# Two 64-wide self-attention blocks: transposed scores and column sums replaced by normalised weights that TensorE turns

## What is computed

```python
q = (xn @ q_w + q_b).reshape(b, s, H, HD).transpose(0, 2, 1, 3)     # H = 16, HD = 64, s = 512
k = (xn @ k_w + k_b).reshape(b, s, H, HD).transpose(0, 2, 1, 3)
v = (xn @ v_w + v_b).reshape(b, s, H, HD).transpose(0, 2, 1, 3)
q, k = _rope(q, theta), _rope(k, theta)                              # B1 only
scores = jnp.einsum('bhqd,bhkd->bhqk', q, k) * scale                 # scale = 1/8
scores = jnp.where(causal, scores, -jnp.inf)                         # B1 only
attn = jax.nn.softmax(scores, axis=-1)
ctx = jnp.einsum('bhqk,bhkd->bhqd', attn, v)
attn_out = ctx.transpose(0, 2, 1, 3).reshape(b, s, H * HD) @ o_w + o_b + xn
```

## Time and profile before

| what | us |
|---|---|
| median of three runs | 2612.14 |
| lowest and highest of them | 2607.64, 2616.47 |
| profiled execution, first to last instruction (its span) | 2602.9 |
| PE busy in it | 2223.6 (85%) |
| DVE busy | 1696.5 (65%) |
| ACT busy | 1135.9 (44%) |
| mean granted TensorE clock | 0.928 of full speed |

### The profile page before, as it was taken

The page is one execution under the profiler, slowest core; times in us unless marked ns, Lnnn a source line. Parts: engine busy times, 40 slices in busy tenths (PEclk is TensorE's granted clock), DMA queues, the critical chain, the costliest instruction groups (busy, mean ns, idle before and its releaser), DMA issues.

```text
span 2602.9 us, 32241 instructions
## 1 busy us (share of the span) xinstructions
PE 2223.6 (85%) x11288; PEld 882.6 (34%) x11288; DVE 1696.5 (65%) x3941; ACT 1135.9 (44%) x1859; POOL 143.0 (5%) x143
## 2 busy tenths in 40 slices
PE   7999979889999898887887888788788878867898
PEld 3333333533333564223323222332322233232433
DVE  5767758646566687765774676577567557754464
ACT  3333323112223333563665466365546636654411
POOL 0000000011110201000000000000000000010000
PEclk9999989789999898888999799799979979988999
DMA  4000000200000100000000010010001000030000
GB/s 145 1 1 1 1 1 1 96 19 1 1 1 1 52 21 25 25 1 25 24 20 1 25 43 1 25 37 7 3 23 43 1 25 26 2 102 1 1 1 8
DMA packets 38032, 54.33 MB, mean 21 GB/s; under 512 B 5073, under 2 KB 34546, under 8 KB 36338
## 3 DMA queue, kind: packets, MB, share of 16 engines
q1 hardware_dynamic: 37874, 52.28, 6.4%
HBM read 32.34 MB, written 0.52 MB: 13 GB/s over the span
## 4 chain that ended last, share of the span: by engine, by line
PE 38%; DVE 10%; ACT 8%; issue 4%; SPq 1%; DMA 0%; ACTq 0%; DVEq 0%
PE ps L2084 7%; PE ps L2064 5%; ACT big L2569 4%; PE ps L2045 4%; DVE C_nm L2746 3%; PE ps L2212 2%; PE ps L2129 2%; PE ps L2319 2%; PE ps L2224 2%; ACT big L2649 2%; PE ps L2315 2%; PE ps L2340 2%; PE ps L2231 2%; PE ps L2240 2%; PE ps L2189 1%
## 5 line engine op out<-in xcount | busy, mean ns | idle before, releaser
L2746 DVE TENSOR_REDUCE C_nm<-ps 128x1 f32<-128x512 f32 x768 | 501.9, 685 | 185.6 <-PE ps L2045 180.9
L2569 ACT ACTIVATE big<-ps 128x512 f32<-128x512 f32 x768 | 427.7, 595 | 234.3 <-PE ps L2064 225.0
L2045 PE MATMUL ps<-C_attn 62*128 62x512 bf16 x768 | 276.5, 417 | 62.6 <-DVE C_nm L2746 51.6
L2064 PE MATMUL ps<-C_attn 64*128 64x512 bf16 x768 | 253.7, 398 | 62.1 <-ACT big L2569 51.8
L2084 PE MATMUL ps<-big,C_attn 128*32 128x512 f32 x1536 | 212.8, 627 | 13.3 <-ACT big L2569 13.3
L2045 PEld LDWEIGHTS ps<-C_attn 62*128 62x128 bf16 x768 | 63.2, 94 | 304.1 <-DVE C_nm L2746 165.7
L2064 PEld LDWEIGHTS ps<-C_attn 64*128 64x128 bf16 x768 | 59.3, 93 | 274.9 <-ACT big L2569 204.1
L2649 ACT ACTIVATE big<-ps,C_biasx 77x512 f32<-77x512 f32 x192 | 115.6, 679 | 56.4 <-PE ps L2216 56.3
L861 DVE TENSOR_REDUCE A_nm<-ps 128x2 f32<-128x1024 f32 x64 | 77.8, 1215 | 85.8 <-PE ps L609 85.5
L787 ACT ACTIVATE A_p<-ps 128x1024 f32<-128x1024 f32 x64 | 65.6, 1025 | 110.2 <-PE ps L637 110.2
L787 ACT ACTIVATE B_p<-ps 128x1024 f32<-128x1024 f32 (+1 forms) x64 | 45.0, 703 | 149.7 <-PE ps L641 149.7
(11 more groups left out here) (414 smaller groups left out, 3787.5 us busy)
## 6 DMA issues: line engine op xcount, KB each, us to landing
C_attn<-C_first SPq DMA_DIRECT2D x144, 128.0 KB, 2.4
C_w<-in_C_w SPq DMA_DIRECT2D x6, 1090.0 KB, 5.0
C_attn<-in_D_ew SPq DMA_DIRECT2D x4, 1536.0 KB, 10.9
big<-in_B_ew SPq DMA_DIRECT2D x8, 514.0 KB
normw_later<-in_norm_w SPq DMA_DIRECT2D x1, 2304.0 KB, 16.3
A_w<-in_A_w SPq DMA_DIRECT2D x2, 1024.0 KB, 11.6
A_w<-in_A_w SPq DMA_DIRECT2D x2, 768.0 KB, 8.6
B_w<-in_B_w SPq DMA_DIRECT2D x1, 1536.0 KB, 11.2
```

Source lines behind the costliest of these rows:

```text
L2045: pe.matmul(ps[:, bank, :], lhsT=qs[side(hp, MAX_ROW), b, 2 * q + pq, t * P:(t + 1) * P], rhs=ks[side(hp, MAX_ROW), b, 2 * q + pq, :], sta ...
L2064: pe.matmul(ps[:, bank, :], lhsT=ks[side(1 - hp, HALF), b, 2 * q + pq, kt * P:(kt + 1) * P], rhs=qs[side(1 - hp, HALF), b, 2 * q + pq, :], ...
L2569: act.activation(prob[:, kt % 2, pq, 1 - hp, :], ps[:, bank, :], ACT.Exp, scale=SCALE)\
L2746: dve.tensor_reduce(nm[:, q % 2, t, pq, hp:hp + 1], ps[:, bank, :], AX.X, ALU.max, negate=True).then_inc(emptied[bank], 1)
```

## The change

`self_attention_block` is rewritten; A1 and B1 both use it. The unit of work is now a **step** i = (unit n, tile t of 128 queries), 64 in all. The scores are made once (`scores`), into one of two pairs of banks. DVE takes the row maxima. ACT takes the exponential of each head's rows by itself, with the negative maximum as its bias and with the row's sum as a second output. DVE inverts the two sums of each row and multiplies the rows by them in place (`weights`). PE turns the normalised rows in blocks of 128 x 128 (`turn`), ACT copies the turned blocks from PSUM (`copy_turned`), and PE makes the weighted sums of the 128 queries (`weigh`), one step behind the turning. ACT copies a unit's context (in B1 it adds the bias), `project_out` makes the output of each unit with tokens as rows, and DVE adds it to y unit by unit (`add_out`).

`split_max`, `turn_max`, `scores_T`, `add_up`, `denominators`, `invert`, `normalise`, `copy_out` and `turn_out` are gone. DVE, not ACT, copies queries and keys in A1 and multiplies the queries by 1/8 on the way; in B1 the tables of the queries carry the 1/8. Three banks (4, 5, 7) form a ring: projections, turned blocks and outputs take the next bank in turn, and PE waits until the bank's last content was taken.

```diff
+            def fill(key):
+                bank = RING[len(turns) % len(RING)]
+                turns.append(key)
+                uses[bank] += 1
+                place[key] = bank, uses[bank]
+                if uses[bank] > 1:
+                    pe.wait_ge(emptied[bank], uses[bank] - 1)
+                return bank
...
+            def turn(i):
+                n, t = divmod(i, TB)
+                pe.wait_ge(p_ready, 2 * (i + 1))
+                for key, heads in turned(i):
+                    bank = fill(key)
+                    for j, h in enumerate(heads):
+                        for kt in range(keys(t) // P):
+                            col = j * keys(t) + kt * P
+                            last = pe.transpose(ps[:, bank, col:col + P], prob[:, i % 2, h, kt * P:(kt + 1) * P],
+                                                m.ident[:])
+                    last.then_inc(filled[bank], 1)
+
+            def weigh(i):
...
+                for kt in range(keys(t) // P):
+                    for h in range(2):
+                        last = pe.matmul(ps[half(h), PV_BANK, t * P:(t + 1) * P], lhsT=v[:, n % 4, kt, half(h)],
+                                         rhs=probT[:, i % 2, kt, h, :], start=kt == 0, stop=kt == keys(t) // P - 1)
...
+            for i in range(STEPS):
+                n, t = divmod(i, TB)
+                if i + 2 < STEPS:
+                    scores(i + 2)
+                turn(i)
+                if i:
+                    weigh(i - 1)
+                if n + 2 < N:
+                    for what in at_step[t]:
+                        project(n + 2, what)
+                if t == TB - 1 and n:
+                    project_out(n - 1)
...
         @block.scalar
+            for i in range(STEPS):
+                n, t = divmod(i, TB)
+                copy_turned(i)
+                if t == 0 and n:
+                    copy_context(n - 1)
+                if t == 2 and n + 2 < N:
+                    copy_v(n + 2)
+                if i + 2 < STEPS:
+                    exps(i + 2)
...
         @block.vector
+            for i in range(STEPS):
+                n, t = divmod(i, TB)
+                if n + 2 < N and t in (1, 2):
+                    for what in at_step[t - 1]:
+                        take(n + 2, what)
+                if i + 2 < STEPS:
+                    row_max(i + 2)
+                if i + 1 < STEPS:
+                    weights(i + 1)
+                if t == 0 and n >= 2:
+                    add_out(n - 2)
```

More of the change, by code:

```diff
@@ new lines, in _, with project @@
+            ring.fill = fill
+            def project(n, what):
+                if n not in begun:
+                    begun.append(n)
+                    for (first, _), loaded in zip(W_PARTS, w_loaded):
+                        if first == n:
+                            pe.wait_ge(loaded, 16)
+                    if n == PAIRS and opening is not None:
+                        drained(pe, "turn_norm")
+                bank = fill((what, n))
+                if what == "v":
+                    for t in range(TB):
+                        last = pe.matmul(ps[:, bank, t * P:(t + 1) * P], lhsT=hT(n)[:, t * P:(t + 1) * P],
+                                         rhs=weight(n, WV), start=True, stop=True)
+                else:
+                    last = pe.matmul(ps[:, bank, :], lhsT=weight(n, column[what]), rhs=hT(n), start=True, stop=True)
+                last.then_inc(filled[bank], 1)
@@ L757, in _ @@
-            weigh(N - 1, TB - 1)
-            project_out(N - 2)
-            denominators(N - 1)
-            project_out(N - 1)
-            if tail is not None:
-                tail.tensor(pe, N, 0, S_BANK)
-            else:
-                for b in range(B):
-                    turn_out(b, S_BANK + b)
+            for what in pieces:
+                project(0, what)
+            for i in range(2):
+                scores(i)
+                project(i, "v")
+            for what in pieces:
+                project(1, what)
@@ new lines, in exps @@
+            def exps(i):
+                n, t = divmod(i, TB)
+                act.wait_ge(max_done, i + 1)
+                if i >= 2:
+                    for key, _ in turned(i - 2):
+                        arrived(act, key)
+                for h in range(2):
+                    act.activation(prob[:, i % 2, h, 0:keys(t)], ps[:, S_BANK + 2 * (i % 2) + h, 0:keys(t)], ACT.Exp,
+                                   bias=nm[:, i % 2, h:h + 1], accum_out=sums[:, i % 2, h:h + 1]).then_inc(exp_done, 1)
@@ new lines, in copy_turned @@
+            def copy_turned(i):
+                n, t = divmod(i, TB)
+                if i >= 2:
+                    act.wait_ge(pv_done, i - 1)
+                for key, heads in turned(i):
+                    bank = arrived(act, key)
+                    out = probT[:, i % 2, 0:keys(t) // P, heads[0]:heads[-1] + 1, :]
+                    act.activation(out.rearrange("p k h q -> p h k q"), ps[:, bank, 0:len(heads) * keys(t)]
+                                   .rearrange("p (h k q) -> p h k q", h=len(heads), q=P), ACT.Copy)\
+                        .then_inc(emptied[bank], 1)
@@ new lines, in weights, with add_out @@
+            def weights(i):
+                n, t = divmod(i, TB)
+                dve.wait_ge(exp_done, 2 * (i + 1))
+                c.after(dve.reciprocal(inv[:, i % 2, :], sums[:, i % 2, :]))
+                for h in range(2):
+                    row = prob[:, i % 2, h, 0:keys(t)]
+                    dve.tensor_scalar(row, row, inv[:, i % 2, h:h + 1], None, ALU.mult).then_inc(p_ready, 1)
+            def add_out(n):
+                bank = arrived(dve, ("out", n))
+                if n % PAIRS:
+                    drained(dve, ("out", n - 1))
+                b = n // PAIRS
+                y = m.y[:, b * TB:(b + 1) * TB, :]
+                dve.tensor_tensor(y, y, ps[:, bank, :].rearrange("p (t d) -> p t d", t=TB), ALU.add)\
+                    .then_inc(emptied[bank], 1)
```

706 lines of the change are left out of this document (238 added, 468 removed).

## The result

| what | us |
|---|---|
| changed kernel, median of four runs (lowest, highest) | 2493.44 (2491.65, 2495.53) |
| kernel before in the same comparison, median of four | 2609.89 (2605.66, 2616.47) |
| ratio, 95% interval | 0.9562 (0.954 to 0.9585) |
| profiled execution after: its own time, its span | 2491.65, 2489.9 |

What follows compares the result with a forecast made beforehand. PE was taken to bound A1 and B1. Gains of 22 + 84 + 1 = 107 us gave a 2496 us span, 2505 as median; with 15 us for changes of shape, 2520 us, range 2480 to 2575.

Steps and rivals of the forecast that it cites:

- the changes of shape: PE's steps in A1 and B1: 0.03 us x 4 x 128 steps, 15 us, added at the end of the sum.
- The second 15 us: PE's steps in both blocks: the whole 0.16 us at each change would make the sum another 15 us longer.
- the sum of the parts: Gains of 22 us in A1, 84 in B1 and 1 in stage C: 107 us off the 2602.9 us span.
- PE's sum as the period: A1 and B1: the sum of PE's work sets a unit's time; step 3.15, units 18.05 and 15.2 us, waits included.
- The ring's wait: PE waits for a bank until DVE adds an output: 1.15 us a unit in A1, 0.4 in B1.
- DVE and ACT hidden: A1: DVE 12.0 and ACT 11.6 us a unit lie under PE's 18, with a step to spare.
- The sines: They run while ACT waits for B0n's DVE chain; without that cover they would cost 5 us.
- heads not side by side: Rival, 832 weighing pairs in A1 and B1: the two heads run one after another, 2633 us; chance 0.06.
- ACT as the bound: Rival, A1 and B1: PE waits for turned blocks from ACT, 48 us more, 2568 us; chance 0.12.
- No ring wait: Rival, A1 and B1: DVE comes earlier, so the wait does not show; 19 us less, 2501 us; chance 0.15.
- Changes of shape eating all: Rival: shape changes and hand-overs, 0.7 us a step over 128 steps, take the whole gain; 2605 to 2620 us; chance 0.04.
- The clock: Rival, new loops: the granted clock falls to 0.5, PE's sums double, over 2800 us; chance 0.03.

Runs made afterwards that it cites:

- every turning twice: Every block of weights turned twice into the same place of the bank, against the changed kernel: 2559.55 us, ratio 0.982 to the kernel before.
- two-row order: Weighted sums of a step made for all key tiles of head 0, then head 1, instead of alternating, against the changed kernel: 2520.69 us, ratio 0.9675.
- real separation: Head 0's weighing put ahead of the turning and head 1's behind it, against the changed kernel: 2579.62 us, ratio 0.9889.

## Why the prediction was right, and where 27 us went

The forecast of 2520 us was 26.6 too slow. Three terms account for it.

- **15 us: the changes of shape, counted twice.** This is the term that failed. The prediction rightly saw that a change has a price (it put 0.13 us; removing one gave 0.15 to 0.20), but it took its terms from rows that had a change at their ends: 1.06 for scores, 1.0 for transposes, 1.09 for weighing, 1.06 for the projection. Without a change these are 0.96, 8 x 0.109, 8 x 0.109 and 0.95, so the four terms held 0.56 us for four changes, 0.14 each: the whole price. The 0.03 for each change, 15 us, added "at the end" were the same microseconds again. The step measured 1.06 + 1.02 + 1.02 + 1.06 = 4.16, under the 4.21 of the terms without that addition. The Trainium skill's page "TensorEngine Tiling (Array Packing)", Tiling Modes (Key Properties), says that a switch of mode drains the engine; the 0.15 to 0.20 us here agree in kind. The second 15 us that the prediction worked out beside it did not come.
- **5.7 us: the offset of the median.** The prediction added 9.2 us to the span, by how one profiled execution of before lay to its median. After, the difference is 2493.44 - 2489.9 = 3.5.
- **5.9 us: the sum of the parts.** A1 gave 25.3 for 22 and B1 85.6 for 84: the weighing took 1.02 and not 1.09, 64 x 0.07 = 4.5 us in A1. That A1's sum came so near is partly luck: its unit was 0.40 us shorter than forecast, 6.4 us in sixteen, and the two waits of 2.3 us with the loss of clock behind one of them took some 4 of these back. Outside the blocks, A2+A3 took 6.6 us more than before, B0n 1.9 less and C 6.6 less (1 expected).

The differences outside the blocks are not the change's as far as these runs show. A2+A3 goes with its granted clock. This was 0.91 in the profile of before, 0.87 in that of the changed kernel, and 0.93 in the shortest (every turning twice), for the same instructions in these two; over all ten profiles A2+A3 is the shorter the higher its clock. Why the clock differed, and what made B0n and C shorter, stays open:

```profile
309.27:483.68 174.41, 149.86 (x749) 66.98 (x749) 108.94 (x174) 47.92 (x67) 0.85 (x4) 0.87 0.00 1
```

```profile
353.29:517.85 164.56, 140.67 (x748) 63.33 (x749) 108.92 (x174) 47.91 (x67) 0.84 (x4) 0.93 0.00 1
```

What held:

- *PE's sum as the period.* Step 3.10 for 3.15, unit 17.65 for 18.05 in A1, 15.17 for 15.2 in B1; doubling a term of it lengthened the blocks by that term.
- *The ring's wait*, found in the order of the code before any trace could show it: 0.86 to 0.93 us a unit in A1 for 1.15, 0.32 in B1 for 0.4, with the addition as the releaser. Missed was the extra fill of the norm's turn, which makes a wait of 2.3 us, twice; the prediction had PE stand "at most about 1 us", and held that against a loss of clock, which then came behind one of the two.
- *DVE and ACT hidden.* DVE 47.26/70 x 17.65 = 11.9 us a unit for 12.0; ACT 10.8 for 11.6. A multiplication took 0.484 for 0.46, a reciprocal of two columns 0.155, an exponential of one head 0.697 for 0.7.
- *The sines* lie in B0n while ACT would wait, and B0n is no longer than before: 26.1 to 28.0 us in the nine kernels with the change, against 28.1.

The bounds that the prediction gives for A1's unit, 15.7 and 21, come out of its own terms as 15.3 and 21.7; its forecast does not rest on them.

The rivals: heads not side by side is refuted, and its price is now measured, 85 us here, with one or two more changes of shape in a step included, rather than 113. ACT as the bound is refuted: even with each copy doubled the unit stays at 17.65. Beside that rival stood the Trainium skill's page "TensorEngine Tiling (Array Packing)", Performance Considerations (PSUM Bottleneck): tiling speeds TensorE and not the emptying of PSUM, and the copy may become the bottleneck. In this kernel it does not: ACT is busy 42.86 of 70 us. No ring wait is refuted by the wait itself. Changes of shape eating all is refuted: with four changes in each of 128 steps at 0.15 to 0.20 they cost an estimated 77 to 102 us in all, but they were in the sum. The clock stayed at 1.00 in the loops but for the one stop above.

## What to carry to other kernels

- When terms of a sum come from rows of a trace, ask what each pitch already contains. A price found by comparing two pitches is inside the larger of them; adding it again is the error made here.
- Before the lengths of a block in two profiles are compared, compare the granted clock of its parts: here 1.5 us at the start of B1 would have been put down to the edits.
- On TensorE order matmuls of one shape next to each other, and write down the whole sequence first, masks included: the same exchange was worth 0.2 us a step in A1 and a quarter of that in B1, where the mask was already such a neighbour.
- A ring of banks ties PE to whichever engine empties a bank, in the order of that engine's own work. Let an engine do first what frees a bank; no other wait took its place here, and it gave 18 to 20 us in the two blocks.

## What the runs showed of the hardware that was not expected

- Matmuls in different halves of the array's columns pass each other: in the two-row order the second head started three records before the first head's row had started its last. So order alone cost 0.49 us a step, and real separation 1.0 us, one more change of shape included. The Trainium skill's page "TensorE: Matmul & The Clock Gate", Part 3 (The mechanism), has matmuls start in program order; these records do not agree.
- A sum as the second output of an exponential is a second instruction on ACT, 0.217 us, 128 times in A1. It overlaps the next exponential in part, so that the two heads of a step take 1.44 us (ACT's rows from 193.19 to 194.63 on the timeline) instead of 2 x (0.697 + 0.217) = 1.83. Here it is hidden.
- The multiplication in place takes 0.484 us in A1, where POOL has nothing to do, and 0.699 in the mean at the same width in B1. Of these 32 in B1, the 18 without an addition of POOL beside them take 0.474 to 0.486, the 14 with one 0.62 to 1.016. One row of B1's timeline, with POOL's addition beside it:

```profile
614.38 1.27 POOL L567 TENSOR_TENSOR B_k<-B_rot 128x512 f32<-128x512 f32 x1 [2.90 <-DVEq L774]
...
614.92 1.41 DVE L795 TENSOR_SCALAR B_p<-B_p,B_inv 128x512 f32<-128x512 f32 x2
```

  The first of the two records takes 1.016 and ends only after POOL's, the second 0.475. The Trainium skill's page "GPSIMD Engine Reference", Specifications, says that the two engines share interfaces to SBUF, and these records agree. The price is half a microsecond a unit in B1, and it is hidden too.
